# Four-layer graph network on one core: another order of TensorE's and VectorE's work in the two convolution edge passes

## The reference

```python
q = (x @ Wq + bq).reshape(n, HEADS, C)
k_j = k[src] + e                     # e = edge_attr @ We, 128 edge features
v_j = v[src] + e
alpha = jnp.einsum('ehc,ehc->eh', q[dst], k_j) / jnp.sqrt(jnp.float32(C))
amax = jax.ops.segment_max(alpha, dst, num_segments=n)
expa = jnp.exp(alpha - amax[dst])
denom = jax.ops.segment_sum(expa, dst, num_segments=n)
attn = expa / (denom[dst] + 1e-16)
out = jax.ops.segment_sum(attn[:, :, None] * v_j, dst, num_segments=n)
```

## Time and profile before

| what | before |
|---|---|
| median of three runs | 13,884.4 us |
| the profiled execution's own time | 13,875.03 us |
| its span | 13,873.3 us |
| granted TensorE clock, mean over the span | 0.778 |
| first convolution pass, first to last scan up | 9,859.2 to 11,719.8 us |
| second convolution pass, first to last scan up | 11,900.3 to 13,760.1 us |

### The profile page before, as it was taken

How to read it: one execution, slowest core, us unless ns; L and a number is a source line. 1 busy time by engine, 2 the same in 40 slices (tenths; PEclk the granted TensorE clock), 3 DMA queues, 4 the chain that set the end, 5 groups by cost and what they waited for, 6 DMA issues and landing times. The chain is left out here.

```text
span 13873.3 us, 209115 instructions
## 1 busy us (share of the span) xinstructions
PE 8685.8 (63%) x52858; PEld 7028.6 (51%) x52859; DVE 10723.6 (77%) x16335; ACT 2809.5 (20%) x4518; POOL 6951.8 (50%) x7719
## 2 busy tenths in 40 slices
PE   4663577767778678773566636773666665666664
PEld 3552255553566446553555524552555554555554
DVE  7666479964899559985888867998677877677777
ACT  0110222223222232220444412221000000000000
POOL 3774057730777227760777706773344443344442
PEclk8555788878788788886888856665788888788887
DMA  4335754437444464451555612222233333333333
GB/s 179 113 112 131 266 165 105 104 53 295 112 105 104 113 260 106 105 93 28 141 147 145 141 23 51 54 54 23 86 96 92 93 95 69 95 93 93 95 93 65
DMA packets 720170, 1523.50 MB, mean 110 GB/s; under 512 B 364796, under 2 KB 416585, under 8 KB 680627
## 3 DMA queue, kind: packets, MB, share of 16 engines
q0 software_dynamic: 306624, 795.04, 24.1%
q1 hardware_dynamic: 413427, 727.07, 15.4%
HBM read 1050.48 MB, written 471.10 MB: 110 GB/s over the span
## 5 line engine op out<-in xcount | busy, mean ns | idle before, releaser
L967 POOL DMA_INDIRECT h<-table,edges_ring x3984 | 3785.5, 950 | 1291.0 <-issue 1161.1
L1146 PE MATMUL bank<-h,edges_onehot 128*128 128x260 f32 (+1 forms) x7968 | 2150.6, 431 | 717.6 <-DVE acc L1307 396.4
L1146 PEld LDWEIGHTS bank<-h,edges_onehot 128*128 128x128 f32 x7968 | 1693.8, 263 | 1130.2 <-DVE acc L1307 458.7
L1241 DVE TENSOR_TENSOR_SCAN bank<-edges_fresh,edges_top,bank 4x1024 f32<-4x1024 bf16 x660 | 1542.0, 2336 | 426.8 <-PE bank L1121 426.8
L967 POOL DMA_INDIRECT edges_rows<-table,edges_ring x1512 | 1492.3, 987 | 465.0 <-issue 415.7
L1121 PE MATMUL bank<-ident,edges_score 128*4 128x128 f32 x5280 | 1017.2, 358 | 953.1 <-DVE edges_score L1271 797.3
L1248 DVE TENSOR_TENSOR_SCAN edges_top<-edges_fresh,bank 4x1024 f32<-4x1024 bf16 x660 | 1497.0, 2268 | 0.2
L956 POOL COPY edges_ring<-src_idx 128x8 uint32 (+1 forms) x440 | 90.7, 207 | 2759.4 <-PE bank L1146 1356.4
L1121 PEld LDWEIGHTS bank<-ident,edges_score 128*4 128x4 f32 x5280 | 495.9, 104 | 1266.9 <-DVE edges_score L1271 841.9
L1307 DVE TENSOR_TENSOR acc<-acc,bank 128x260 f32 (+1 forms) x2640 | 919.8, 348 | 206.1 <-DVE acc L1297 59.8
L2010 POOL DMA_INDIRECT rec<-dst,slots x782 | 797.1, 1019 | 433.6 <-issue 433.2
(11 more groups left out here) (345 smaller groups left out, 16680.7 us busy)
## 6 DMA issues: line engine op xcount, KB each, us to landing
table<-x SPq DMA_DIRECT2D x154, 1040.0 KB, 7.9
edge_score<-edge_feat SPq DMA_DIRECT2D x220, 512.0 KB, 3.7
table<-h SPq DMA_DIRECT2D x77, 1040.0 KB, 7.9
table<-source_typed_rows SPq DMA_DIRECT2D x63, 1040.0 KB, 8.1
h<-table,edges_ring POOLq DMA_INDIRECT x3984
edge_feat<-edge_score SPq DMA_DIRECT2D x110, 512.0 KB, 3.0
dst_row<-dst_rows SPq DMA_DIRECT2D x71, 704.0 KB, 4.2
buf<-rec SPq DMA_DIRECT2D x44, 840.0 KB, 5.2
```

Source lines behind the costliest of these rows:

```text
L967: pool.indirect_dma_start(out=rows[s % R][:, j, :], out_offset=None, in_=table, in_offset=bass.IndirectOffsetOnAxis(ap=ring[:, s * ST + j: ...
L1146: ins = pe.matmul(sum_b[k % 3], onehot[s][:, j, :], rows[s][:, j, A0:W], start=j == k * GT, stop=j == (k + 1) * GT - 1)
L1241: v.tensor_tensor_scan(score_b[0:HEADS, :], fresh[s][:, 0:SLOTS_SB], score_b[0:HEADS, :], top[1 - s][:, SLOTS_SB - 1:SLOTS_SB], ALU.add, A ...
```

## The change

In the two convolution passes:

- TensorE: a step begins with the 4 loads of the bins of n, then half 0 is spread, then come sum groups 0 to 2 of o, `turn_top` of m, sum group 3, half 1, the flip of the next superblock's one-hot, and `turn_scores` of n. Before, the step began with groups 0 to 2, then came the flip of n, the loads, group 3, half 0, `turn_top`, half 1 and `turn_scores`. The first one-hot is flipped ahead of the loop.
- ScalarE: the copy of the flipped one-hot stands at the end of a step, for the next superblock.
- VectorE: `weigh_rows` stands behind `make_score`, at the end of the step. The one-hot of the next superblock is made between the two halves' work, ahead of `subtract_top`, and reads the places from SBUF instead of PSUM.

In all six attention passes VectorE reads two bins after `scan_up` and two after `scan_down` instead of four after `scan_up`. TensorE's order with `conv` None is the same as before.

```diff
@@ TensorE
 def step(n, m, o):
-    bins = []
-    if o:
+    if o and conv is None:
         for k in range(GPS - 1):
             sum_group(o, k)
+    if n and conv is None:
+        flip_onehot(n)
     if n:
-        flip_onehot(n)
-        bins += [load_bin(pe, g, number(n), k) for k in range(GPS)]
+        bins = load_bins(pe, g, number(n))
+    if n and conv is not None:
+        spread_half(n, 0, bins)
+    if o and conv is not None:
+        for k in range(GPS - 1):
+            sum_group(o, k)
+    if m and conv is not None:
+        turn_top(m)
     if o:
         sum_group(o, 3)
     if n and conv is None:
         spread_dst(n, bins)
-    if n and conv is not None:
-        spread_half(n, 0, bins)
-    if m:
+    if m and conv is None:
         turn_top(m)
     if n and conv is not None:
         spread_half(n, 1, bins)
+        flip_onehot(after(n))
     if n:
         turn_scores(n)
+if conv is not None:
+    flip_onehot((0, 0))
 superblocks(pe, step)
@@ ScalarE: the copy of the flipped one-hot, now keep_flipped_onehot(n)
 def step(n, m, o):
-    if n:
-        (wait for the flip, copy)
+    if n and conv is None:
+        keep_flipped_onehot(n)
     ...
+    if n and conv is not None:
+        keep_flipped_onehot(after(n))
@@ VectorE
-make_onehot(v, g, number(n), onehot[n[1]], onehot_made, place_b)
+make_onehot(v, g, number(n), onehot[n[1]], onehot_made, place_b if conv is None else None)
 ...
 if m:
     scan_up(m)
 if o:
-    bins = load_bins(v, g, number(o))
+    bins = [load_bin(v, g, number(o), k) for k in range(2)]
     scale_sums(o, c, bins)
     add_sums(o, 0, bins)
 if m:
     scan_down(m)
 if o:
+    bins += [load_bin(v, g, number(o), k) for k in range(2, GPS)]
     add_sums(o, 1, bins)
 if m:
     find_fall(m)
 if o:
     add_sums(o, 2, bins)
 if n and conv is not None:
     convolve_half(n, 0, c)
+    onehot_ahead(after(n))
 if m and conv is not None:
     subtract_top(m)
 if o and conv is not None:
     add_sums(o, 3, bins)
-if m and conv is not None:
-    weigh_rows(m)
 if n and conv is not None:
-    onehot_ahead(after(n))
     convolve_half(n, 1, c)
 if n:
     make_score(n, c)
+if m and conv is not None:
+    weigh_rows(m)
```

More of the change, by code:

```diff
@@ L1180, in narrow_ahead, with keep_flipped_onehot @@
                                    ).then_inc(narrow_made, 1)
-                def step(n, m, o):
-                    if n:
[L1184 to L1191, removed]
+                def keep_flipped_onehot(n):
+                    u, s = number(n), n[1] % 2
+                    act.wait_ge(onehot_flipped, u + 1)
+                    if conv is None:
+                        hold(act, dst_spread, u - 1)
+                    else:
+                        hold(act, half_ready, 2 * (u - 1))
+                    act.activation(flippedT[s][:, :, :].rearrange("p t c -> p (t c)"),
+                                   narrow_b[:, :] if conv is None else flip_b[:, :], ACT.Copy).then_inc(flipped_kept, 1)
+                def step(n, m, o):
+                    if n and conv is None:
+                        keep_flipped_onehot(n)
                     if m:
@@ L1202, in step @@
                         narrow_ahead(after(n))
+                    if n and conv is not None:
+                        keep_flipped_onehot(after(n))
+                if conv is not None:
+                    keep_flipped_onehot((0, 0))
                 if conv is None:
```

## The result

The kernel after took 14,596.5 us (median, 14,591.6 to 14,603.9) beside 13,886.1 us for the kernel before: the ratio is 1.0511, 95% interval 1.0493 to 1.0529. The profiled execution's span is 14,598.8 us. The forecast was 14,325 us, the range 13,950 to 14,640; the time is that of the rival "both halves slow in nearly all steps", 14,605 us.

What follows compares the result with a forecast made beforehand. GpSimd paces relational passes, VectorE is busiest in convolution passes; only the latter can move. Pieces 6.0 + 5.09 + 2.24 + 3.26 = 16.6 us, with slow clock 19.15 against 17.07, over 218 steps add 453 us: 14,325 us, range 13,950 to 14,640.

Steps and rivals of the forecast that it cites:

- both halves slow in nearly all steps: Rival, convolution passes: spreading half 0 slowly lengthens step and pauses; 3.35 us more in 218 steps, 14,605 us; chance 0.17.
- The loads: TensorE, convolution step: four bin loads run from score + 0.1 for 3.0 us, behind the score wait, ahead of half 0.
- The flip costed at nothing: TensorE, behind half 1: 8 transposes, 1.04 us under VectorE's reduction; at the lower clock a 0.8 us delay, also covered.
- one sign that failed: VectorE, convolution passes: its wait for the turned scores was to be under 0.8 us a step, from 1.93.
- Score to first addition: First piece of a convolution step: 6.0 us instead of 5.87 at full clock; half 0 at the lower clock adds 2.2.
- The second piece: Convolution step on VectorE, from first addition of sums to half 0 taken: order kept, 5.09 us.
- The third piece: Convolution step, half 0 taken to start on half 1: 2.24 us instead of 2.63; lower clock adds 1.6.
- The share of slow steps: Convolution steps: half 0 slow in four of five, half 1 in one of two; 16.6 us becomes 19.15.
- my case of both: Convolution step with half 0 and half 1 both at the lower clock: 20.4 us, against 16.6 at full clock.
- The argument against that case: TensorE, convolution step: after a slow and therefore full half 0 the clock should be back for what follows.
- The other passes and the split: VectorE's split loads: 0 in the other four attention passes, bounds -0.1 and +0.1 us on 440 steps; nothing in convolution steps.
- faster, by the loads: Rival: TensorE reads bins while waiting for the score; first piece 4.3 to 5.1, step 14.9 to 15.7, 13,570 us; chance 0.05.

Runs made afterwards that it cites:

- e1: Kernel after with TensorE's four bin loads of a convolution step moved ahead of the next one-hot's flip; 13,902.3 us, ratio to the kernel before 1.0008.
- e2: Kernel after with each TensorE bin load of a convolution step made twice, the second set unused; 15,070 us, ratio to the kernel before 1.0853.
- e3: Kernel after with 12 unused transposes behind half 1, the turned scores and sum groups 0 to 2 in convolution steps; 13,885.8 us, ratio to before 0.9998.
- e4: Kernel before with only VectorE's bin loads split two and two in all six attention passes; 13,883.8 us, ratio to the kernel before 0.9999.
- e6: Kernel after with 16, 5, 14 and 16 unused transposes filling all TensorE pauses in convolution steps; ratio 0.9733 to the kernel before in its job.
- e10: The kernel of e6 once more, in a later job; ratio 0.973 to the kernel before in that job.

## Why the prediction was right, and where its size was off

*The loads.* Right in place and length: 2.9 us, behind the wait for the scores, half 0 released by issue; e1 and e2 confirm that they are on the path. I had them at score + 0.1, and in three steps of four they start at score + 0.2. In the fourth, and the step shown above is one, they start at score + 0.6. The program loop has a body of four steps, and there it turns: its compare and branch (L900) stand between the wait and the loads. The next step, with its score at 10,635.55, has none:

```profile
L900 PEldq COMPARE_BRANCH  x1: 215/215/215, 10614.9 to 10614.9; - x1
...
L936 PEldq TENSOR_LOAD <-bin_row x4: 297/298/305, 10635.7 to 10638.0; - x4
```

Steps in which the loop turns take 20.8 us and the others 20.3 on the mean, and in e3 at full clock it is 17.3 against 16.65 to 16.8. The prediction has no term for the loop.

*The flip costed at nothing* held, as the scan covers it. At the lower clock its 8 transposes take 1.97 us and hold the score transposes back to score + 0.56 in every kind of step. The loads don't stand behind it: in the next step they start at 10,635.7, and the score transposes at 10,636.12. The delay shows in one sign that failed: the wait for the turned scores was to fall under 0.8 us a step and is 1.46. It also fills part of the pause behind the turned scores, which was to be some 2.5 us and is 1.0.

*Score to first addition:* 8.2 us with half 0 slow (6.0 + 2.2), measured 8.11 on the mean and 10,623.21 - 10,614.72 = 8.49 in the step shown, where the loop turns.

*The second piece,* 5.09: measured 5.11, and 5.10 in the step before the one shown, from the first addition at 10,602.41 to half 0 taken at 10,606.82 + 0.69 = 10,607.51.

*The third piece,* 2.24 or 3.84 at the lower clock: measured 3.94 on the mean, and 10,611.46 - 10,607.51 = 3.95. The weighing moved away, and TensorE is last, as forecast.

*The share of slow steps* is the term that was mis-sized. I took half 0 slow in 0.8 of the steps and half 1 in 0.5, 19.15 us; the step is 20.35, my case of both (20.4): half 0 is granted under 0.6 in 96% and half 1 in 99% of the steps. The shares were a choice, and the time lies inside the range because the range was drawn to take in the case of both. The argument against that case, that a full slow half 0 brings the clock back for what follows, was true for the sums (12 matmuls in 1.82 us) and not for half 1: between them lie a wait for the fall of 2.0 us and the ten tiny matmuls of `turn_top`.

*The other passes and the split:* 0, as forecast, and e4 shows 0 for the convolution passes too.

*Slips that the forecast doesn't rest on.* GpSimd's waits on others in the row are 5.4 us (3.7 + 1.7) and not 7.4. The rival "faster, by the loads" has a step of 14.9 to 15.7, which is 1.4 to 2.2 us under 17.07, and was priced at 1.4 alone: its middle is near 13,490 us and not 13,570. e1 has its first piece (5.12, at the upper end of 4.3 to 5.1) and not its third.

*What I didn't foresee* is where the kernels come to rest when the loss is undone. Before, e3, e4 and the second pass of e1 mean 17.05 to 17.07 us with four different patterns of waits, single steps from 16.1 to 18.5 (score to score, without the first and last three of a pass), and granted clocks from 0.80 to 0.98. For e3 the parts are known: 178 steps at 16.83 and 40 at 18.1. Against before, e1 gains 0.61 in the first piece and loses 0.71 in the third, e3 loses 0.51 and gains 0.49, e4 gains 0.98 and loses 0.96 in the second and third. In the second pass of e1 the steps repeat in fours for most of the pass (17.08, 17.13, 17.04, 17.01), the number of the loop's body. That the clock's changes thereby pull the mean to one value is my reading; e6 and e10 were to test it, and their jobs didn't allow it. Why it is 17.06 stays open, and so does what a kernel with early loads and a full clock would take where the kernel before takes 13,885 us.

## What to carry to other kernels

Register loads in front of an instruction stand behind every wait that the sequencer passes before them: four of them are 2.9 us here, free beside a running engine and on the path behind a wait. A loop's branch stands there too, so a step that is read as typical should be compared with its neighbours. Where a matmul engine has pauses, price a new order at both clocks and ask which burst stands behind the longest thin stretch: it should be one that nobody waits for. And work that covered a wait uncovers it when it moves: VectorE's weighing had covered part of half 1's spreading.

## What the runs showed of the hardware

- The mean step stayed at 17.05 to 17.07 us in four kernels whose common short steps differ by 0.9 us (16.1 in e4, 17.0 in the second pass of e1).
- The same kernel took 13,886 to 13,889 us in two jobs and 16,008 to 16,047 us in three later ones, one of them on the chip of a fast job, with unchanged durations of single operations (scan up 2,343 ns in both) and longer waits between them.
- Four register loads with their checks took 2.9 us in a row on TensorE's sequencer, of which a load instruction itself is 0.30 us (half of the floor that the prediction cites), and a second four behind them (e2) put half 0 off by 2.6 us more.
- Where the program loop turned, once in four steps, TensorE's loads started 0.4 us later (0.6 behind the score and not 0.2), and the step was 0.5 us longer.
- A longer pause did not go with a lower clock: 3.9 us behind the turned scores in e2 with 0.68 over the pass, 1.0 us in the kernel after with 0.59.
- Unused transposes raised the granted clock from 0.59 to 0.98 and saved 711 us of 14,597 (e3).
